# Gate weights move into the sorted rows, a token's two expert results become neighbours, and the last stage is rewritten without loops

## The reference

```python
gating = softmax(X @ Wg + bg)                        # [tokens, 8]
top_k_indices = argsort(gating)[..., -2:]
h = silu((X @ W1[e] + b1[e]) * (X @ W3[e] + b3[e]))  # per expert e, 512 wide
expert_outputs = h @ W2[e] + b2[e]                   # 256 wide
mixed = sum over the token's two experts of gate weight * expert output
x = layernorm(X + mixed @ Wf + bf)
```

## Time and profile before

| | us |
|---|---|
| median of 3 runs | 1953.55 (1951.57 to 1959.17) |
| the profiled execution | 1948.98 |
| its span in the trace | 1947.3 |
| PE busy | 1737.1 (89%) |
| VectorE busy | 1262.3 (65%) |
| ScalarE busy | 882.6 (45%) |
| GpSimd busy | 366.4 (19%) |

### The profile page before, as it was taken

One profiled execution on the slowest core, in us unless ns is written; L12 is line 12 of the kernel. 1 busy time (PEld: TensorE's weight loads), 2 busy tenths in 40 slices (PEclk: granted clock), 3 DMA queues, 4 the chain that ended last, 5 costly groups with the idle time before them and its releaser, 6 DMA issues.

```text
span 1947.3 us, 28314 instructions
## 1 busy us (share of the span) xinstructions
PE 1737.1 (89%) x9130; PEld 920.4 (47%) x9131; DVE 1262.3 (65%) x2992; ACT 882.6 (45%) x1035; POOL 366.4 (19%) x478
## 2 busy tenths in 40 slices
PE   6998479999999999999999999977639999999965
PEld 3444234444444444444444444426525666666644
DVE  3677867777777777777777777516525555555536
ACT  2677524455555555555455554544311221221236
POOL 0111211111121111211211112103572111111111
PEclk9999768899999999999999999997759999999988
DMA  3366434011021020110201103016521111111144
GB/s 102 137 238 236 179 129 147 7 36 70 8 73 39 15 90 7 57 50 7 99 12 39 67 7 121 13 60 204 205 95 38 47 43 48 44 43 49 44 132 151
DMA packets 99497, 155.30 MB, mean 80 GB/s; under 512 B 10752, under 2 KB 60736, under 8 KB 99008
## 3 DMA queue, kind: packets, MB, share of 16 engines
q1 hardware_dynamic: 84928, 122.53, 18.9%
q0 software_dynamic: 14464, 31.40, 4.6%
HBM read 87.90 MB, written 65.35 MB: 79 GB/s over the span
## 4 chain that ended last, share of the span: by engine, by line
PE 70%; DVE 8%; ACT 7%; issue 6%; DMA 5%; POOL 2%; SPq 1%; another core or an unknown queue 0%; ACTq 0%; DVEq 0%; POOLq 0%
PE att_ps_s L884 22%; PE exp_ps_h L1564 13%; PE att_ps_o L903 12%; PE att_ps_m L862 10%; PE exp_ps_y L1582 6%; ACT att_probs L931 3%; DMA out_parts<-att_out_t 2%; PE pre_ps_q L311 2%; PE exp_ps_t L1572 2%; PE pre_ps_h L311 1%; DVE att_maxima L945 1%; DMA k_parts<-pre_waves 1%; PE exp_ps_x L1553 1%; POOL sorted_rows L1449 1%; DMA route_a_inv<-inv_rows 1%
## 5 line engine op out<-in xcount | busy, mean ns | idle before, releaser
L931 ACT ACTIVATE att_probs<-att_ps_s 128x1024 f32<-128x1024 f32 (+3 forms) x640 | 563.7, 895 | 484.4 <-PE att_ps_s L884 476.5
L884 PE MATMUL att_ps_s<-att_queries,att_keys 49*128 49x512 f32 (+3 forms) x2560 | 632.8, 561 | 20.9 <-ACT att_probs L931 11.4
L945 DVE TENSOR_REDUCE att_maxima<-att_ps_m 128x1 f32<-128x512 f32 x768 | 487.1, 684 | 153.6 <-PE att_ps_m L862 148.6
L862 PE MATMUL att_ps_m<-att_keys,att_queries 48*128 48x512 f32 (+3 forms) x1280 | 506.5, 605 | 24.1 <-DVE att_maxima L948 15.9
L862 PEld LDWEIGHTS att_ps_m<-att_keys,att_queries 48*128 48x128 f32 x1280 | 197.7, 193 | 315.8 <-DVE att_maxima L945 141.4
L884 PEld LDWEIGHTS att_ps_s<-att_queries,att_keys 49*128 49x128 f32 x2560 | 242.9, 191 | 127.3 <-ACT att_probs L931 85.4
L948 DVE CUSTOM_DVE_ANT_0 att_ps_m<-att_ps_m,att_future 128x128 f32<-128x128 f32 (+3 forms) x512 | 240.3, 514 | 73.4 <-PE att_ps_m L862 72.1
L903 PE MATMUL att_ps_o<-att_probs,att_values 128*32 128x512 f32 (+3 forms) x2560 | 269.3, 535 | 11.1 <-POOL att_probs L1034 11.1
L1564 PE MATMUL exp_ps_h<-keep_w,exp_rows_t 128*128 x568 | 257.4, 596 | 5.5 <-DVE exp_rows_t L1598 5.5
L1640 ACT ACTIVATE exp_hidden<-exp_product 128x512 f32<-128x512 f32 x71 | 44.8, 632 | 343.7 <-DVE exp_product L1623 343.7
L1034 POOL TENSOR_SCALAR_AFFINE_SELECT att_probs<-att_probs 128x512 f32<-128x512 f32 x128 | 81.1, 634 | 491.3 <-ACT att_probs L931 491.2
(11 more groups left out here) (179 smaller groups left out, 1458.6 us busy)
## 6 DMA issues: line engine op xcount, KB each, us to landing
att_queries<-q_parts SPq DMA_DIRECT2D x64, 192.0 KB
att_keys<-k_parts SPq DMA_DIRECT2D x64, 192.0 KB
exp_rows<-sorted_rows SPq DMA_DIRECT2D x71, 129.0 KB, 2.3
v_rows<-pre_v_sb SPq DMA_DIRECT2D x8, 1024.0 KB, 7.1
q_parts<-pre_waves SPq DMA_DIRECT2D x16, 512.0 KB, 4.2
k_parts<-pre_waves SPq DMA_DIRECT2D x16, 512.0 KB, 5.8
att_values<-v_rows SPq DMA_DIRECT2D x32, 256.0 KB
out_parts<-att_out_t POOLq DMA_DIRECT2D x32, 256.0 KB, 6.0
```

Source lines behind the costliest of these rows:

```text
L862: pe.matmul(take()[:, 0:width], queries[g % 2][half, c, r, P * q:P * q + P], keys[g % 2][half, k, r, 0:width], start=True, stop=True).then ...
L884: mm = pe.matmul(score_tile(unit, first, last)[:, e], keys[g % 2][half, k // TPC, r, P * (k % TPC):P * (k % TPC) + P].bitcast(F32), querie ...
L931: act.activation(probs[:, step % PROBS, DUO * r:DUO * r + DUO, first:last], score_tile(unit, first, last), ACT.Exp, scale=SCALE).then_inc( ...
L945: dve.tensor_reduce(to, buf[:, 0:width], AX.X, ALU.max).then_inc(s_mr, 1)
```

## The change

The rows in `x1`, and so in `sorted_rows`, grow to 260 floats: both gate weights stand in them, and the number that they carry is 2t+1 instead of t: rows 2t and 2t+1 of `expert_rows` are now the results of token t's first and second expert. In `experts` VectorE has one more small instruction for each tile, which chooses the gate, and ScalarE multiplies the result by it in place; GpSimd's store waits for that. In `finish` a chunk is loaded as one transfer of 1 MB into one of four buffers, VectorE adds neighbouring rows in two halves of a chunk, ScalarE's weighing is gone, `mixed` has one buffer instead of two, and the lists of the engines are new. `Norm` gets two sets of its small tiles there. The last chunk is stored in two halves.

```diff
-ROW, TOKEN, FIRST_EXPERT = D + 2, D, D + 1
+ROW, FIRST_ROW, FIRST_EXPERT, FIRST_WEIGHT, SECOND_WEIGHT = D + 4, D, D + 1, D + 2, D + 3
...
-    if loops < 2:
+    if unrolled or loops < 2:
...
-        if since(i, 1):
-            act.wait_ge(self.s_done, i * TPC)
-        act.activation(self.rstd[:, :], self.var, ACT.Sqrt, bias=eps).then_inc(self.s_std, 1)
+        if i >= self.depth:
+            act.wait_ge(self.s_done, (i - self.depth + 1) * TPC)
+        act.activation(self.rstd[:, i % self.depth], self.moments[:, i % self.depth, 1], ACT.Sqrt, bias=eps).then_inc(self.s_std, 1)
...
-                    top = weight[:, r, mine]
+                    top = x1[:, mine, FIRST_WEIGHT + r]
...
-                dve.tensor_scalar(second[:, p:p + 1], rows[:, p, FIRST_EXPERT:ROW], column(tile_number), float(T),
-                                  ALU.not_equal, ALU.mult).then_inc(s_second, 1)
-                dve.wait_ge(s_second, s + 1)
+                dve.tensor_scalar(is_first[:, mine], rows[:, p, FIRST_EXPERT:FIRST_EXPERT + 1], column(tile_number), None,
+                                  ALU.is_equal).then_inc(s_which, 1)
+                dve.wait_ge(s_which, s + 1)
                 if since(s, 4):
                     dve.wait_ge(s_out[p], 16 * (s >> 2))
-                dve.scalar_tensor_tensor(dest[:, p:p + 1], rows[:, p, TOKEN:TOKEN + 1], second[:, p:p + 1], column(own_places),
-                                         ALU.add, ALU.min).then_inc(s_dest, 1)
+                dve.scalar_tensor_tensor(gate[:, mine], rows[:, p, FIRST_WEIGHT:FIRST_WEIGHT + 1], is_first[:, mine],
+                                         rows[:, p, SECOND_WEIGHT:SECOND_WEIGHT + 1], ALU.mult, ALU.max).then_inc(s_gate, 1)
+                dve.scalar_tensor_tensor(dest[:, mine], rows[:, p, FIRST_ROW:FIRST_ROW + 1], is_first[:, mine], column(own_places),
+                                         ALU.subtract, ALU.min).then_inc(s_dest, 1)
...
-            pipelined(act, SLOT_TILES, [(activate, 1), (keep_hidden, 2)], body=4)
+
+            def weigh(s, p):
+                act.wait_ge(s_r, s + 1)
+                act.wait_ge(s_gate, s + 1)
+                act.activation(result[:, p], result[:, p], ACT.Copy, scale=gate[:, p:p + 1]).then_inc(s_gated, 1)
+            pipelined(act, SLOT_TILES, [(activate, 1), (keep_hidden, 2), (weigh, 3)], body=4)
...
-                pool.wait_ge(s_r, s + 1)
+                pool.wait_ge(s_gated, s + 1)
...
-            sp.dma_start(wf[:, :], Wf.rearrange("(k p) n -> p k n", p=P)).then_inc(s_w, 16)
-
-            def load(i, p):
-                if since(i, 2):
-                    sp.wait_ge(s_mix, (i - 1) * TPC)
-                for r in range(TOPK):
-                    sp.dma_start(picked[:, p, r], at(rows_in[r], i)).then_inc(s_pick[p], 16)
-            pipelined(sp, NCH, [(load, 0)])
+            sp.dma_start(picked[:, 0, 0:half], rows_in[0][:, 0:half]).then_inc(s_begin, 16)
+            sp.dma_start(picked[:, 0, half:TPC], rows_in[0][:, half:TPC]).then_inc(s_pick[0], 16)
+            sp.dma_start(wf[:, :], Wf.rearrange("(k p) n -> p k n", p=P)).then_inc(s_wf, 16)
+            for i in range(1, NCH):
+                if i >= 4:
+                    sp.wait_ge(s_mix, 2 * (i - 3))
+                sp.dma_start(picked[:, i % 4], rows_in[i]).then_inc(s_pick[i % 4], 16)
...
+            for i in range(NCH):
+                parts = [slice(0, TPC)] if i < NCH - 1 else [slice(0, half), slice(half, TPC)]
+                for part in parts:
+                    pool.wait_ge(norm.s_done, i * TPC + part.stop)
+                    pool.dma_start(rows_out[i][:, part], normed[:, i % 2, part]).then_inc(s_out[i % 2], 16)
...
-            pe.wait_ge(s_w, 16)
+            pe.wait_ge(s_wf, 16)
 
             def turn(i, p):
-                pe.wait_ge(s_mix, i * TPC + TPC)
-                if since(i, 1):
+                if i >= 1:
                     pe.wait_ge(s_mt, i)
-                turn_rows(pe, ps_m, mixed[:, p], ident[:, :]).then_inc(s_mp, 1)
+                for t in range(TPC):
+                    pe.wait_ge(s_mix, 2 * i + t // half + 1)
+                    for k in range(DK):
+                        mm = pe.transpose(ps_m[:, k, t * P:(t + 1) * P], mixed[:, t, k * P:(k + 1) * P], ident[:, :])
+                mm.then_inc(s_mp, 1)
...
-            pipelined(pe, NCH, [(turn, 0), (project, 1)])
+            pipelined(pe, NCH, [(turn, 0), (project, 1)], unrolled=True)
...
-            pipelined(act, NCH, [(normalise, 4), (weigh_first, 0), (keep_mixed, 1), (lambda i, p: norm.root(act, i, eps[:, 0:1]), 3)])
+            pipelined(act, NCH, [(keep_mixed, 0), (lambda i, p: norm.root(act, i, eps[:, 0:1]), 1), (normalise, 2)], unrolled=True)
...
             def mix(i, p):
-                dve.wait_ge(s_pick[p], 16 * TOPK * ((i >> 1) + 1))
-                for t in range(TPC):
-                    dve.wait_ge(s_first, i * TPC + (t + 1))
-                    dve.scalar_tensor_tensor(mixed[:, p, t], picked[:, p, 1, t], gate(1, i, t), mixed[:, p, t],
-                                             ALU.mult, ALU.add).then_inc(s_mix, 1)
+                if i >= 1:
+                    dve.wait_ge(s_mp, i)
+                for part in (slice(0, half), slice(half, TPC)):
+                    if i == 0 and part.start == 0:
+                        dve.wait_ge(s_begin, 16)
+                    elif part.start == (half if i == 0 else 0):
+                        dve.wait_ge(s_pick[i % 4], 16 * (i // 4 + 1))
+                    dve.tensor_tensor(mixed[:, part], picked[:, i % 4, part, 0], picked[:, i % 4, part, 1], ALU.add).then_inc(s_mix, 1)
...
-            pipelined(dve, NCH, [(mix, 0), (scale_and_shift, 3), (residual, 2)])
+            pipelined(dve, NCH, [(mix, 0), (residual, 1), (scale_and_shift, 2)], unrolled=True)
```

More of the change, by code:

```diff
@@ L111, with pipelined @@
 Mixed = namedtuple("Mixed", "s_out s_x1")
-def pipelined(eng, count, stages, body=2):
+def pipelined(eng, count, stages, body=2, unrolled=False):
     deepest = max(lag for _, lag in stages)
@@ L1076, with __init__ @@
 class Norm:
-    def __init__(self, n, region):
+    def __init__(self, n, region, depth=1):
+        self.depth = depth
         self.stats = n.sb(region, "stats", [P, TPC, 6])
-        self.moments = n.sb(region, "moments", [P, 4, TPC])
-        self.mean_twice, self.var, self.m2, self.gap = (self.moments[:, i] for i in range(4))
-        self.rstd = n.sb(region, "rstd", [P, TPC])
+        self.moments = n.sb(region, "moments", [P, depth, 4, TPC])
+        self.rstd = n.sb(region, "rstd", [P, depth, TPC])
         self.s_stats = n.sem("stats_ready")
@@ L1092, in statistics @@
     def statistics(self, dve, i, rows):
+        mean_twice, var, m2, gap = (self.moments[:, i % self.depth, j] for j in range(4))
         for t in range(TPC):
@@ L1158, in __init__ @@
         self.reached = n.sb(small, "reached", [P, NE])
-        self.token = n.sb(small, "token", [P, NT])
+        self.first_row = n.sb(small, "first_row", [P, NT])
         self.ones_f = n.sb(small, "ones_f", [P, NE])
@@ L1482, in experts @@
         rows_t = n.sb(small, "rows_t", [P, 2, DK, P])
-        second = n.sb(small, "second", [P, 4])
+        is_first = n.sb(small, "is_first", [P, 4])
+        gate = n.sb(small, "gate", [P, 4])
         dest = n.sb(small, "dest", [P, 4], U32)
@@ L1682, in finish @@
         normed = n.sb(room, "normed", [P, 2, TPC, D])
[L1683 to L1685 removed]
+        shift = n.sb(room, "shift", [P, 2, TPC])
+        norm = Norm(n, room, depth=2)
         ps_m = n.ps("ps_m", [P, DK, CH])
         ps_y = [n.ps(f"ps_y{p}", [P, TPC, D]) for p in range(2)]
[L1689 to L1691 removed]
+        s_wf = n.sem("weight_loaded")
+        s_begin = n.sem("first_rows_picked")
+        s_pick = [n.sem(f"rows_picked{i}") for i in range(4)]
         s_shift = n.sem("shift_ready")
@@ L1700, in finish @@
         rows_out = out.rearrange("b (c t p) d -> (b c) p t d", p=P, t=TPC)
-        rows_in = [expert_rows[r * T:(r + 1) * T].rearrange("(c t p) d -> c p t d", p=P, t=TPC) for r in range(TOPK)]
-        def gate(r, i, t):
-            return weight[:, r, i * TPC + t:i * TPC + t + 1]
+        rows_in = expert_rows[0:TOPK * T].rearrange("(c t p r) d -> c p t r d", p=P, t=TPC, r=TOPK)
+        half = TPC // 2
         @block.sync
@@ L1725, in _ @@
-            pipelined(pool, NCH, [(store, 0)])
-            for p in range(2):
-                pool.wait_ge(s_out[p], 16 * NCH // 2)
+            for i in range(NCH):
[3 more added lines that the diff above has]
+                    pool.dma_start(rows_out[i][:, part], normed[:, i % 2, part]).then_inc(s_out[i % 2], 16)
+            pool.wait_ge(s_out[0], 16 * (NCH // 2))
```

89 lines of the change are left out of this document (40 added, 49 removed).

## The result

The changed kernel takes 1990.47 us (median of 4, 1987.37 to 1993.96) where the kernel before takes 1952.56 (median of 4): a ratio of 1.0183, interval 1.0155 to 1.0211. It is slower, by 37.9 us between the medians.

The account below looks back on a forecast made before the run. The prediction took TensorE to bound the expert stage and VectorE the last stage's steady part. Its terms, -1.5 + 24.3 + 13.2 - 0.3 + 0.9 = +36.6 on 1953.55, gave 1990.2 us, range 1972 to 2001.

Parts of the forecast that it names:

- The circle: Last stage, steady part: mix, turn, projection, residual, next mix run serially, period 9.1 us at full clock; six periods cost +24.3.
- The clock: Last stage: TensorE idles some 4.4 us each period, so most bursts begin at low clock; 2.2 for each of six, +13.2.
- The route row: Route-stage profile row: after 3.86 us idle the turn still took 1.10 us, read as full clock, against the clock term.
- The join: Expert stage to last stage: the first residual gains 1.5 us, between 0.5 lost and 3.5 gained.
- The term of +0.55: Last tile of the expert stage: the added weighing has no cover there and delays the join by 0.55 us.
- Seventh to eighth residual: Last stage: the eighth residual follows the seventh by 3.7 us instead of 3.99, -0.3.
- The end: Behind the eighth residual: last normalised row at 7.85 instead of 6.2 us, +1.7; half-length last transfer -0.8; together +0.9.
- Route and experts: Route: longer rows cost 0, between -1 and +1; expert stage: extra VectorE and ScalarE work hidden beside TensorE, 0.
- The clock holds: Rival, last stage: TensorE keeps full clock, the 13.2 falls away; +23.4, 1977 us, chance 0.21.
- The clock never comes back up: Rival, last stage: every burst of about 4.6 us doubles; +54, 2007 us, chance 0.10.
- the circle is open: Rival, last stage: projection ready when VectorE reaches the residual, VectorE alone sets the period, 4.95 us; 1952 us, chance 0.06.
- no room in the expert stage: Rival, expert stage: extra VectorE work delays each tile and binds TensorE; up to +16, about 2004 us with the forecast, chance 0.05.

Follow-up runs that it names:

- run 5: The changed kernel with 8 extra, unused TensorE matmul calls of 128x256 after each projection but the last: 1980.84 us, ratio 1.0139 to the kernel before.
- run 1: The changed kernel with TensorE's last-stage list turned round, project i-1 before turn i: 1957.97 us, ratio 1.0034 to the kernel before.
- run 2: The changed kernel with VectorE's residual and shift at the old lags, ScalarE's root and normalisation one later, normalisation before root: 1951.18 us, ratio 0.9986.
- run 12: The kernel before with only VectorE's and ScalarE's last-stage lists changed to the new kind, residual at lag 1, written out: 2005.81 us, ratio 1.0246.
- run 10: As run 2, without the weighing in the expert stage (ScalarE's multiplication, VectorE's gate choice and their waits), output a plain sum: 1942.73 us, one time.
- run 6: The changed kernel with VectorE's shift ahead of the residual and ScalarE's normalisation ahead of the root, residual still at lag 1: 1985.13 us, one time.
- run 9: As run 2, with rows of 259 floats instead of 260, the second gate weight left out of the row: 1950.87 us, one time.

## Why the prediction was right, point by point

- **The circle.** Predicted +24.3, measured with the clock held up 54.1 - 30.34 = +23.8 (run 5). The idle brackets, the two engines as each other's releasers, and runs 1, 2 and 12 are what the prediction asked for.
- **The clock.** Predicted +13.2, between 0 and 17; measured 10.6, or 1.8 us for each burst instead of 2.2. That TensorE's idle time costs clock was right; the size was somewhat too large, and the account of how a burst begins was only half right. I expected that most bursts begin low. Of the seven turns from the second chunk on, four did and took 1.94 us; the other three, 1.81, 1.22 and 1.63 us, began at 1.00 after 4.12 and 4.41 us of idle time, and the clock fell to 0.50 within the turn or at the start of the projection. By the rule of the Trainium skill ("TensorE: Matmul & The Clock Gate", HAM oscillation) each would begin at half clock; four of the seven agree, three don't. The cost is there all the same, since the low stretch then falls on the projection.
- **The route row was misread.** The row of 3.86 us was taken as one that "was passed at full clock". Its turn was, but the clock fell right behind it:

```profile
1369.60:1373.60 4.00, 0.14 (x2) 0.07 (x2) 3.75 (x13) 2.07 (x4) 3.09 (x4) 1.00 0.65 242
1375.20:1379.20 4.00, 3.47 (x17) 3.47 (x17) 0.44 (x1) 3.34 (x4) 1.99 (x3) 0.50 1.05 381
1379.20:1385.90 6.70, 6.67 (x17) 5.02 (x17) 4.47 (x25) 0.52 (x2) 2.88 (x3) 0.55 0.83 325
```

The projection of that burst took 6.70 us in place of 3.47. Nor did "nearly every burst of the route stage" begin low: of six turns between 1344 and 1417 us four took 1.09 or 1.10 us, and the projections behind three of these took 5.86 to 6.70 us. So this row was no support for the rival that the clock holds, and a short turn is no sign of a burst at full clock: the granted clock has to be read to the end of the burst.

- **The join.** Predicted -1.5, measured -1.2 in this pair; against the second trace of the kernel before it would be -2.1, so the size is known to about 1 us. The term of +0.55 is right (runs 2 and 10, 4.3 against 3.8). The first turn began when Wf had landed, as predicted.
- **Seventh to eighth residual.** Predicted -0.3, measured +1.8: a wait that the sum left out. I named two things that residual 7 waits for and not the third, chunk 5's normalisation behind root 6 in ScalarE's list (run 6). In the six periods the same wait is hidden in the circle.
- **The end.** Predicted +0.9, measured +1.0: the last normalised row comes 7.7 us behind the eighth residual (predicted 7.85), 1.5 later than before, and what follows it is 0.5 shorter. Run 6 shows the 2.07 us of normalise 6 behind root 7 as predicted.
- **Route and experts.** Predicted 0, between -1 and +1 in the route. The route was 4.0 us shorter, which can't be told from its scatter. The steady expert stage is 402.0 us in every trace, with and without weighing. Its start was not foreseen: see below.
- **The rivals.** "The clock holds" was run 5's result and not the changed kernel's. "The clock never comes back up", "the circle is open" and "no room in the expert stage" are each contradicted by a window above. The sum of the last one was off as well: with its full +16 it is 2006, not 2004. That the median came out within 1 us of the forecast is partly luck: the clock term was 2.6 too large, the missed wait of 2.1 made up for it, and the start of the expert stage and the scatter ahead of it are in no term.

## What to carry to other kernels

In a pipeline written as in-order lists, compare the lag of a step on one engine with the lag of its producer on another. Where the consumer sits just one position behind and both lists contain the step that feeds the next round, write the round down as a cycle and add its terms; if nothing of another item stands in it, the period is the sum and not the largest. Deeper load buffers and lighter steps don't help against that, and the idle time that it makes on TensorE can be paid a second time through its clock (10.6 us here, on top of 23.8). Check each two-tile resource against the consumer's list too, since that is where the small wait hid.

## What was not expected of the hardware

- **GpSimd's addition depends on the distance between rows.** The same instruction on 128x1024 takes 2217 to 2226 ns with rows of 258 or 259 floats and 2396 to 2400 with 260 (ten traces with 260, one with 259, three with 258). Why is open.
- **VectorE's operation on two SBUF tiles can stretch while GpSimd adds.** The product of 128x512 takes 0.69 us in the steady stage. At the start, beside GpSimd's eight additions, the timeline of before shows

```profile
1456.54 1.20 DVE L1623 TENSOR_TENSOR exp_product<-exp_left,exp_right 128x512 f32<-128x512 f32 x1
...
1462.76 1.82 DVE L1623 TENSOR_TENSOR exp_product<-exp_left,exp_right 128x512 f32<-128x512 f32 x1
```

and that of after

```profile
1462.32 2.93 DVE L1632 TENSOR_TENSOR exp_product<-exp_left,exp_right 128x512 f32<-128x512 f32 x1
```

The biases added from PSUM in between keep their 0.69 us. The amount varies with the moment: in run 5 the first product beside the additions took 0.69 us too and the next one 2.35. From the first turn to the first result it is 21.7 us in both traces of the kernel before and 23.1 to 26.3 in the changed kernel and its variants, but run 12, with rows of 258 floats, has 25.5 and run 9 with 259 has 24.2. In all the traces above 24 a second or third multiplication by W1 and W3 took 5.4 to 6.4 us instead of 3.7, at a clock below 1.00. So in these traces the start takes the changed kernel and its variants 1.4 to 4.6 us longer than those two of the kernel before, and how much of it is the row and how much is the phase of the clock is open.
